# Key maximum taken pair by pair into a PSUM bank, with the engine orders rewritten

## Chip, cores and metric

The program runs on one core of one Trainium2 chip. The metric is the device time of one execution in microseconds (us). Three executions of the kernel before took 1970.22, 1972.08 and 1973.30 us; the median is 1972.08 us.

## What is computed

The reference is one gated cross-attention block and a small gated LoRA mixture behind it:

```
q = layernorm(x) @ wq          # x: 8 batches x 56 tokens x 512; 32 query heads of 128
k = ctx @ wk ; v = ctx @ wv    # ctx: 8 x 1500 x 512; 8 key heads, each shared by 4 query heads
q, k = rope(q), rope(k)
attn = softmax(q k^T / sqrt(128) + mask)      # over the 1500 keys
x = x + tanh(g0) * ((attn v) @ wo)
x = x + tanh(g1) * ffn(layernorm(x))          # 4 LoRA experts, top 2
```

Everything is float32. Large products are made of three fp32r matmuls (hi*hi, hi*lo, lo*hi), for which each operand is split into a high and a low part.

## The kernel before

Three stages follow one another: the query projection (up to about 120 us), the attention stage (to about 1835 us for its first 63 steps), and the output projection with the expert layer. The change is in the attention stage. It has 64 steps, one for each batch `b` (8) and key head `g` (8). In a step 1500 keys stand in 12 tiles of 125 keys on partitions, taken as 6 pairs, and the 4 heads x 56 queries are 224 columns.

The work of a step, by the names used in the order tables:

- `S0`..`S5` (TensorE, `scores`): the scores of one pair of tiles, 6 matmuls into one of two PSUM banks (`t_banks`). A bank is free again when VectorE has read it (semaphore `t_free`).
- `mask0`..`mask5` (VectorE, `add_mask`, L1059): adds the mask and stores the pair in `weights` (SBUF, 125 x 448).
- `max0`, `max1` (VectorE, L1068 and L1077): two row reductions over the stored pairs give `key_max` (125 x 224).
- `MT` (TensorE, L902) transposes `key_max` into `m_bank`; `rows` (VectorE, L1082) reduces it to one maximum for each query; `MB` (TensorE, L909) spreads that back over the key partitions into `m_bank`.
- `sub0`..`sub2` (VectorE, L1089) subtract it, `exp0`..`exp2` (ScalarE, L800) exponentiate, `add1`..`add5` and `total` (GpSimd, L718, L725) add the weights up.
- `PV0`..`PV5` (TensorE, L929) multiply the weights with `v`, `SUM` (L918) spreads the sums, `inv` and `norm` (VectorE, L1096, L1102) divide. A `z` in front of a word marks work of the step before: PV, SUM, inv and norm run one step late.
- `K00`..`K23` (TensorE, L840) project the next step's keys in 3 chunks of 4 parts; `swap` and `K` (ScalarE, L752, L757), `cos`, `sin`, `rot` (VectorE, L1000, L1005, L1014) and `klo` (GpSimd, L687) rotate and split them. `V00`..`V51` (TensorE, L857) project values for a pair of key heads, `V` on ScalarE (L774) stores them.
- `C0`..`C11` and `B0`, `B1` in the last step of a batch: the context and the mask of the next batch are transposed through the same two `t_banks` (L868, L877), with `C` on ScalarE (L761) and on VectorE (L1019) behind.

Nothing is scheduled at run time. Each engine executes a list written out in the tables `PE_STEP`, `ACT_STEP`, `DVE_STEP` and `POOL_STEP`, one entry for each kind of step. The kinds of a batch are zero, odd, even, odd, even, odd, pre, turn; in the last batch the last two are pre_last and last. An engine runs its list in order and waits at an instruction until its semaphores are reached, so whatever stands behind a waiting instruction waits too. A fill of a `t_banks` bank has to have the same place among the fills in the TensorE table and in the VectorE table.

Of the kernel before, what the change touches and what calls it, by code (L numbers as in the profile page):

```python
# [11 lines left out]
AX_X = mybir.AxisListType.X  # L12
# [4 lines left out]
HKV, REP, DH = 8, 4, 128  # L17
# [8 lines left out]
ST = 125  # L26
# [509 lines left out]
def attention_part(nc, ctx, query, shared, cT, ctx_in, mask, wo, q_dram, attn_dram):  # L536
# [50 lines left out]
    steps2 = HKV // 2  # L587
    ADDS = PT - 1
    GROUP = PT // GROUPS
    SHIFTED = PT - GROUP  # L590

    def c_stage_ready(eng, b, m):

# [930 lines left out]
```

## Time and profile before

| | |
|---|---|
| median of three runs | 1972.08 us |
| profiled execution, its own time | 1971.75 us |
| its span, first to last instruction | 1970.0 us |
| TensorE (PE) busy | 1910.2 us, 97% |
| VectorE (DVE) busy | 1530.4 us, 78% |
| ScalarE (ACT) busy | 781.0 us, 40% |
| GpSimd (POOL) busy | 747.5 us, 38% |
| granted TensorE clock, mean | 0.995 |

Matmuls overlap in the trace: one is shown for 0.27 us while the next starts 0.11 us after it. A busy share of 97% therefore does not say how many matmul slots were lost; the distance between the starts of neighbouring matmuls does. PEld is the loading of weights for the matmul behind it, and its waits are shown apart.

### The profile page before, as it was taken

What the parts mean: (1) busy time and instruction counts of PE and PEld (TensorE: products, weight loads), DVE (VectorE), ACT (ScalarE), POOL (GpSimd) and SP (SyncE); (2) the same over time, 40 slices, a digit from 0 to 9 for tenths busy, and PEclk for the clock granted to TensorE, in tenths of its full rate; (3) what the DMA queues carried; (4) which work ended last, traced back from release to release, by engine and by line L of the source; (5) the groups of instructions that cost most, each with busy time, mean ns of one, the idle gap of its engine ahead of it and who ended that gap; (6) DMA issues with size and microseconds to landing.
All of it is one profiled execution on the core that took longest, in us unless ns stands there. A gap on an engine that the chain in (4) does not pass through costs nothing. (4 is left out here: it accounts for less than half of the span.)

```text
span 1970.0 us, 32471 instructions
## 1 busy us (share of the span) xinstructions
PE 1910.2 (97%) x12452; PEld 1776.9 (90%) x12452; DVE 1530.4 (78%) x1822; ACT 781.0 (40%) x1242; POOL 747.5 (38%) x611
## 2 busy tenths in 40 slices
PE   7989999999999999999999999999999999999798
PEld 7879999999999998999899998999899999999786
DVE  6767788788787888778878788787887878778644
ACT  5643334433344334344343343334433334334422
POOL 5513334433343343443244432444234442344500
PEclk9999999999999999999999999999999999999998
DMA  6620001100010001000010001000010000100270
GB/s 223 246 93 22 23 11 34 41 26 10 21 38 30 17 8 41 31 26 10 24 36 31 16 8 41 31 26 10 24 42 25 16 13 21 48 10 8 85 227 19
DMA packets 54806, 84.31 MB, mean 43 GB/s; under 512 B 11684, under 2 KB 30244, under 8 KB 54664
## 3 DMA queue, kind: packets, MB, share of 16 engines
q1 hardware_dynamic: 53656, 75.92, 12.0%
q10 hardware_dynamic: 1008, 6.42, 0.8%
q8 instruction: 98, 1.61, 0.3%
q14 instruction: 44, 0.36, 0.1%
HBM read 66.62 MB, written 15.71 MB: 42 GB/s over the span
## 5 line engine op out<-in xcount | busy, mean ns | idle before, releaser
L687 POOL TENSOR_TENSOR k_lo<-k_work,k_hi 128x500 fp32r<-128x500 f32 x192 | 255.9, 1333 | 569.0 <-ACT k_hi L757 540.9
L752 ACT ACTIVATE k_work<-low_banks 64x500 f32<-64x500 f32 x384 | 223.7, 582 | 581.3 <-PE low_banks L840 575.9
L857 PE MATMUL low_banks<-wv_hi,cT_hi 128*125 128x256 f32 x1536 | 438.3, 285 | 0.0
L857 PE MATMUL low_banks<-wv_lo,cT_hi 128*125 128x256 f32 x1536 | 431.8, 281 | 0.0
L857 PE MATMUL low_banks<-wv_hi,cT_lo 128*125 128x256 f32 x1536 | 431.3, 281 | 0.0
L1059 DVE TENSOR_TENSOR weights<-t_banks,mask_keys 125x448 f32<-125x448 f32 x384 | 236.0, 622 | 162.6 <-PE t_banks L891 161.5
L929 PE MATMUL o_bank<-weights,v 125*128 125x224 f32 x1536 | 337.2, 353 | 0.0
L718 POOL TENSOR_TENSOR key_sum<-key_sum,weights 125x448 f32<-125x448 f32 x256 | 313.7, 1225 | 32.0 <-POOL key_sum L718 1.8
L840 PE MATMUL low_banks<-cT_hi,wk_hi 128*128 128x500 f32 x768 | 322.6, 420 | 0.0
L840 PE MATMUL low_banks<-cT_lo,wk_hi 128*128 128x500 f32 x768 | 298.3, 388 | 0.0
L840 PE MATMUL low_banks<-cT_hi,wk_lo 128*128 128x500 f32 x768 | 298.3, 388 | 0.0
L857 PEld LDWEIGHTS low_banks<-wv_hi,cT_lo 128*125 128x125 f32 x1536 | 285.4, 186 | 3.6
L857 PEld LDWEIGHTS low_banks<-wv_hi,cT_hi 128*125 128x125 f32 x1536 | 285.4, 186 | 3.4
L857 PEld LDWEIGHTS low_banks<-wv_lo,cT_hi 128*125 128x125 f32 x1536 | 285.3, 186 | 0.0
L929 PEld LDWEIGHTS o_bank<-weights,v 125*128 125x128 f32 x1536 | 273.5, 190 | 3.8
L718 POOL TENSOR_TENSOR key_sum<-weights 125x448 f32<-125x448 f32 x64 | 74.3, 1162 | 490.4 <-ACT weights L800 490.1
L891 PE MATMUL t_banks<-q_hi,k_hi 128*125 128x224 f32 x768 | 234.8, 306 | 3.1 <-DVE weights L1059 1.2
L1089 DVE TENSOR_TENSOR weights<-weights,m_bank 125x896 f32<-125x896 f32 x192 | 199.9, 1079 | 31.5 <-PE m_bank L909 31.5
L1068 DVE TENSOR_REDUCE weights<-weights 125x224 f32<-125x1792 f32 x64 | 214.5, 3352 | 1.7
L891 PE MATMUL t_banks<-q_lo,k_hi 128*125 128x224 f32 x768 | 209.1, 272 | 0.0
L891 PE MATMUL t_banks<-q_hi,k_lo 128*125 128x224 f32 x768 | 209.0, 272 | 0.0
L1005 DVE TENSOR_TENSOR k_work<-k_work,k_tables 128x500 f32<-128x500 f32 x192 | 165.0, 859 | 46.3 <-ACT k_work L752 46.3
(140 smaller groups left out, 3081.4 us busy)
## 6 DMA issues: line engine op xcount, KB each, us to landing
stage<-in_ctx_dram SPq DMA_DIRECT2D x72, 250.0 KB
attn_by_head<-o_sum SPq DMA_DIRECT2D x65, 112.0 KB, 1.7
wq_raw<-in_L_xattn_wq_dram SPq DMA_DIRECT2D x7, 1024.0 KB, 7.2
q_raw<-q_by_head SPq DMA_DIRECT2D x64, 112.0 KB, 2.0
head_rows<-in_ctx_dram SPq DMA_DIRECT2D x24, 250.0 KB
stage<-in_L_xattn_wo_dram SPq DMA_DIRECT2D x4, 1024.0 KB, 5.3
k_work<-in_L_xattn_wo_dram SPq DMA_DIRECT2D x4, 1024.0 KB, 5.5
q_by_head<-head_rows ACTq DMA_DIRECT2D x4, 896.0 KB, 6.1
```

The source lines that it names most:

```text
L687: nc.gpsimd.tensor_tensor(k[1][:, c * SC:(c + 1) * SC], k_rot[:, s], f32(k[0][:, c * SC:(c + 1) * SC]), ALU.subtract).then_inc(k_lo, 1)
L718: nc.gpsimd.tensor_tensor(key_sum[:, :, :], so_far, pair_weights(n, j), ALU.add).then_inc(p_added, 1)
L752: nc.scalar.activation(k_swap[lo * HALF:(lo + 1) * HALF, s], k_banks[(1 - lo) * HALF:(2 - lo) * HALF, s, 0:SC], ACT.Copy).then_inc(k_swapp ...
L840: mm = nc.tensor.matmul(k_banks[:, s, 0:SC], w[0][a][:, d, g * DH:(g + 1) * DH], cT[m][:, d, c * SC:(c + 1) * SC], start=(d == 0 and n == ...
L857: mm = nc.tensor.matmul(v_banks[0:ST, v_item(pair, m) % 2, t * PAIR:(t + 1) * PAIR], cT[a][:, d, tile * ST:(tile + 1) * ST], w[1][mv][:, d ...
L891: mm = nc.tensor.matmul(t_banks[0:ST, item % 2, t * GQ:(t + 1) * GQ], k[a][:, tile], q[m][:, :], start=(n == 0), stop=(n == len(PASSES) - 1))
L929: mm = nc.tensor.matmul(o_acc, v[n // 2 % 2][:, 2 * j + t, (n % 2) * DH:(n % 2 + 1) * DH], probs[:, t], start=(j == 0 and t == 0), stop=(j ...
L1005: nc.vector.tensor_tensor(k_swap[:, s], k_swap[:, s], tables[:, 1, c * SC:(c + 1) * SC], ALU.mult).then_inc(k_sined, 1)
L1059: nc.vector.tensor_tensor(pair_weights(n, j).rearrange(four, h=REP), t_banks[0:ST, item % 2, 0:2 * GQ].rearrange("p (t h s) -> p t h s", t ...
L1068: nc.vector.tensor_reduce(weights[:, NT, :], pair_weights(b * HKV + g, 0, SHIFTED).rearrange("p t q -> p q t"), AX_X, ALU.max).then_inc(ma ...
L1089: nc.vector.tensor_tensor(group, group, max_b[:, None, :].broadcast_to([ST, 2 * GROUP, GQ]), ALU.subtract).then_inc(p_shifted, 1)
```

## The change

Instead of two reductions over stored tiles, the running maximum is updated pair by pair. `max1` takes the elementwise maximum of pairs 0 and 1 and writes it (125 x 448) into `m_bank`; `max2` to `max4` take the maximum of `m_bank` and the next pair and write it back; `max5` writes into `key_max`, now two halves of 224 columns; `half` takes the maximum of these halves. `MT` reads the first half. `weights` loses its spare tile, in which the partial maximum stood. `MT` no longer waits for `p_shifted`; `max1` waits for it instead.

```diff
-    weights = sb("weights", [ST, 2 * NT + 1, GQ])
+    weights = sb("weights", [ST, 2 * NT, GQ])
-    key_max = sb("key_max", [ST, GQ])
+    key_max = sb("key_max", [ST, 2, GQ])
+    max_so_far = m_bank[0:ST, 0:2 * GQ].rearrange("p (t q) -> p t q", t=2)
...
-            nc.vector.tensor_reduce(weights[:, NT, :], pair_weights(b * HKV + g, 0, SHIFTED).rearrange("p t q -> p q t"),
-                                    AX_X, ALU.max).then_inc(max_begun, 1)
...
-            nc.vector.tensor_reduce(key_max[:, :], weights[:, first:first + 2 * GROUP + 1, :].rearrange("p t q -> p q t"),
-                                    AX_X, ALU.max).then_inc(max_ready, 1)
+        def max_part(b, g, j, last):
+            n = b * HKV + g
+
+            dve.wait_ge(t_free, t_item(b, g, "S", j, last) + (RING + 1))
+            if j == 1:
+                so_far = pair_weights(n, 0)
+                if n:
+
+                    dve.wait_ge(p_shifted, n * GROUPS)
+            else:
+                so_far = max_so_far
+                dve.wait_ge(max_steps, n * (PT - 1) + (j - 1))
+            out = key_max[:, :, :] if j == PT - 1 else max_so_far
+            nc.vector.tensor_tensor(out, so_far, pair_weights(n, j), ALU.max).then_inc(max_steps, 1)
+
+        def max_half(n):
+            dve.wait_ge(max_steps, (n + 1) * (PT - 1))
+            nc.vector.tensor_tensor(key_max[:, 0], key_max[:, 0], key_max[:, 1], ALU.max).then_inc(max_ready, 1)
```

All tables but `first` are rewritten (`last` on VectorE alone). Of TensorE's, the even and the turn step; of ScalarE's, pre_last, whose `K2` moves behind `V5` and `exp2`:

```diff
 PE_STEP
-    "even": ("zPV0 S0 S1 zPV1 S2 zPV2 S3 S4 zPV3 K00 zPV4 zPV5 S5 zSUM K01 K02 K03 MT K10 K11 K12 MB V30 K13 V31 "
-             "V40 K20 K21 K22 K23 V41 V50 V51"),
+    "even": ("S0 S1 zPV0 S2 S3 zPV1 S4 zPV2 zPV3 S5 K00 zPV4 K01 K02 K03 zPV5 MT K10 K11 K12 MB zSUM K13 K20 K21 "
+             "V30 V31 V40 V41 K22 K23 V50 V51"),
-    "turn": ("S0 S1 zPV0 S2 S3 zPV1 C0 S4 C1 zPV2 zPV3 S5 zPV4 C2 C3 zPV5 zSUM B0 B1 K00 C4 K01 K02 K03 MT C5 C6 "
+    "turn": ("S0 S1 zPV0 S2 S3 zPV1 C0 S4 zPV2 C1 S5 zPV3 zPV4 C2 C3 zPV5 zSUM MT B0 B1 K00 C4 K01 K02 K03 C5 V00 "
 ACT_STEP
-    "pre_last": "Q swap0 swap1 exp0 K0 exp1 exp2 V3 swap2 wo0 K1 V4 K2 V5 attn0",
+    "pre_last": "Q swap0 swap1 K0 V3 exp0 exp1 swap2 wo0 K1 V4 V5 exp2 K2 attn0",
```

VectorE's program in an even step (head 2 of the first batch), from the first mask to `rows`, before:

```order
L1059 TENSOR_TENSOR weights<-t_banks,mask_keys 125x448 [waits p_weighed,p_added,t_ready,t_free]
L1059 TENSOR_TENSOR weights<-t_banks,mask_keys 125x448 [waits t_ready] x3
L1068 TENSOR_REDUCE weights<-weights 125x224 [waits key_max_ready,t_free]
L1059 TENSOR_TENSOR weights<-t_banks,mask_keys 125x448 [waits t_ready] x2
L1077 TENSOR_REDUCE key_max<-weights 125x224 [waits max_begun,t_free]
L1082 TENSOR_REDUCE row_max<-m_bank 112x2 [waits max_turned]
```

and after, where L1057 is the mask, L1074 a maximum of a pair and L1078 the maximum of the halves:

```order
L1057 TENSOR_TENSOR weights<-t_banks,mask_keys 125x448 [waits p_weighed,p_added,t_ready,t_free]
L1057 TENSOR_TENSOR weights<-t_banks,mask_keys 125x448 [waits t_ready] x4
L1074 TENSOR_TENSOR m_bank<-weights 125x448 [waits p_shifted,t_free]
L1074 TENSOR_TENSOR m_bank<-m_bank,weights 125x448 [waits max_steps,t_free] x3
L1057 TENSOR_TENSOR weights<-t_banks,mask_keys 125x448 [waits t_ready]
L1074 TENSOR_TENSOR key_max<-m_bank,weights 125x448 [waits max_steps,t_free]
L1078 TENSOR_TENSOR key_max<-key_max 125x224 [waits max_steps]
L1082 TENSOR_REDUCE row_max<-m_bank 112x2 [waits max_turned]
```

Behind the last mask stood one reduction; now two shorter operations stand there, and four maxima stand between the fifth mask and the sixth.

VectorE's program in the turn step of the first batch, from the first mask to the mask copies, before (L1019 is the low part of a context tile):

```order
L1059 TENSOR_TENSOR weights<-t_banks,mask_keys 125x448 [waits p_weighed,p_added,t_ready,t_free]
L1059 TENSOR_TENSOR weights<-t_banks,mask_keys 125x448 [waits t_ready] x3
L1019 TENSOR_TENSOR cT_lo<-t_banks,cT_hi 128x4x125 [waits c_hi_ready]
L1059 TENSOR_TENSOR weights<-t_banks,mask_keys 125x448 [waits t_ready]
L1068 TENSOR_REDUCE weights<-weights 125x224 [waits key_max_ready,t_free]
L1019 TENSOR_TENSOR cT_lo<-t_banks,cT_hi 128x4x125 [waits c_hi_ready]
L1059 TENSOR_TENSOR weights<-t_banks,mask_keys 125x448 [waits t_ready]
L1019 TENSOR_TENSOR cT_lo<-t_banks,cT_hi 128x4x125 [waits c_hi_ready] x2
L1024 COPY mask_keys<-t_banks 125x336 [waits t_ready] x2
L1077 TENSOR_REDUCE key_max<-weights 125x224 [waits max_begun,t_free]
```

and after, its first twelve rows (L1017 is the low part of a context tile):

```order
L1057 TENSOR_TENSOR weights<-t_banks,mask_keys 125x448 [waits p_weighed,p_added,t_ready,t_free]
L1057 TENSOR_TENSOR weights<-t_banks,mask_keys 125x448 [waits t_ready]
L1074 TENSOR_TENSOR m_bank<-weights 125x448 [waits p_shifted,t_free]
L1057 TENSOR_TENSOR weights<-t_banks,mask_keys 125x448 [waits t_ready]
L1074 TENSOR_TENSOR m_bank<-m_bank,weights 125x448 [waits max_steps,t_free]
L1057 TENSOR_TENSOR weights<-t_banks,mask_keys 125x448 [waits t_ready]
L1074 TENSOR_TENSOR m_bank<-m_bank,weights 125x448 [waits max_steps,t_free]
L1017 TENSOR_TENSOR cT_lo<-t_banks,cT_hi 128x4x125 [waits c_hi_ready]
L1057 TENSOR_TENSOR weights<-t_banks,mask_keys 125x448 [waits t_ready]
L1074 TENSOR_TENSOR m_bank<-m_bank,weights 125x448 [waits max_steps,t_free]
L1017 TENSOR_TENSOR cT_lo<-t_banks,cT_hi 128x4x125 [waits c_hi_ready]
L1057 TENSOR_TENSOR weights<-t_banks,mask_keys 125x448 [waits t_ready]
```

The long reduction that stood between the fifth mask and the second context tile is gone, and two maxima now stand in front of the fourth mask, where none stood.

TensorE's program around `MT` in the same even step, before:

```order
L840 MATMUL low_banks<-cT_hi,wk_hi 128x500
L840 MATMUL low_banks<-cT_hi,wk_lo 128x500
L840 MATMUL low_banks<-cT_lo,wk_hi 128x500
L902 MATMUL m_bank<-ident,key_max 112x125 x2
L840 MATMUL low_banks<-cT_hi,wk_hi 128x500
```

and after (L841 is the key projection, L927 PV, L900 `MT`):

```order
L841 MATMUL low_banks<-cT_hi,wk_hi 128x500
L841 MATMUL low_banks<-cT_hi,wk_lo 128x500
L841 MATMUL low_banks<-cT_lo,wk_hi 128x500
L927 MATMUL o_bank<-weights,v 128x224 x2
L900 MATMUL m_bank<-ident,key_max 112x125 x2
L841 MATMUL low_banks<-cT_hi,wk_hi 128x500
```

`MT` now stands behind the last PV, and `SUM` has gone from in front of it to behind `MB`.

## Rows read from the trace of the kernel before

**Rows 1.** Windows, one whole batch: busy us and instructions of each engine

```profile
556.96:775.72 218.76, 215.67 (x1448) 201.97 (x1447) 177.10 (x207) 85.59 (x140) 84.49 (x73) 1.00 0.08 25
```

**Rows 2.** Waits of TensorE: us in total, times, longest

```profile
PEld m_bank L902 <- DVE key_max L1077: 18.1, 17, 1.2
...
PEld t_banks L868 <- DVE cT_lo L1019: 16.3, 21, 1.1
PEld t_banks L891 <- DVE weights L1059: 6.0, 17, 1.3
```

**Rows 3.** Timeline of PE, even step around MT: start, us, [idle before]

```profile
620.04 0.39 PE L840 MATMUL low_banks<-cT_hi,wk_lo 128*128 128x500 f32 x1
620.27 0.39 PE L840 MATMUL low_banks<-cT_lo,wk_hi 128*128 128x500 f32 x1
621.29 0.43 PE L902 MATMUL m_bank<-ident,key_max 125*112 125x125 f32 x2 [0.62 <-DVE key_max L1077]
```

**Rows 4.** Timeline of PE, odd step, from S1 to S2

```profile
637.72 0.27 PE L891 MATMUL t_banks<-q_lo,k_hi 128*125 128x224 f32 x1
638.09 0.37 PE L891 MATMUL t_banks<-q_hi,k_hi 128*125 128x224 f32 x1
```

**Rows 5.** Timeline of PE, turn step, from PV1 to C2

```profile
525.83 0.93 PE L929 MATMUL o_bank<-weights,v 125*128 125x224 f32 x4
526.60 0.59 PE L868 MATMUL t_banks<-ident,stage 125*128 125x125 f32 x4
...
527.46 0.27 PE L891 MATMUL t_banks<-q_hi,k_lo 128*125 128x224 f32 x1
527.57 0.27 PE L891 MATMUL t_banks<-q_lo,k_hi 128*125 128x224 f32 x1
528.59 0.65 PE L868 MATMUL t_banks<-ident,stage 125*128 125x125 f32 x4 [0.75 <-DVE cT_lo L1019]
...
532.93 1.18 PE L868 MATMUL t_banks<-ident,stage 125*128 125x125 f32 x8 [0.76 <-DVE cT_lo L1019]
```

**Rows 6.** Groups of VectorE by form: busy us, mean ns, idle before

```profile
L1059 DVE TENSOR_TENSOR weights<-t_banks,mask_keys 125x448 f32<-125x448 f32 x384 | 236.0, 622 | 162.6 <-PE t_banks L891 161.5
L1068 DVE TENSOR_REDUCE weights<-weights 125x224 f32<-125x1792 f32 x64 | 214.5, 3352 | 1.7
L1077 DVE TENSOR_REDUCE key_max<-weights 125x224 f32<-125x1120 f32 x64 | 137.5, 2149 | 1.1
L1029 DVE TENSOR_TENSOR q_lo<-q_raw,q_hi 128x224 fp32r<-128x224 f32 x64 | 44.4, 693 | 8.9 <-ACT q_hi L767 8.9
L1102 DVE TENSOR_TENSOR o_sum<-o_bank,inv_b 128x224 f32<-128x224 f32 x64 | 24.6, 385 | 1.1
L514 DVE TENSOR_TENSOR q_banks<-q_banks,q_cos_t 128x448 f32<-128x448 f32 x32 | 19.9, 623 | 0.0
```

**Rows 7.** Timeline of DVE and POOL, one even step: the same operation twice

```profile
625.61 0.67 DVE L1005 TENSOR_TENSOR k_work<-k_work,k_tables 128x500 f32<-128x500 f32 x1
...
629.70 1.66 DVE L1005 TENSOR_TENSOR k_work<-k_work,k_tables 128x500 f32<-128x500 f32 x1
...
629.67 2.70 POOL L718 TENSOR_TENSOR key_sum<-key_sum,weights 125x448 f32<-125x448 f32 x2
```

**Rows 8.** Timeline of PE and DVE, start of a zero step

```profile
556.96 0.26 PE L891 MATMUL t_banks<-q_hi,k_hi 128*125 128x224 f32 x1
...
557.86 0.62 DVE L1059 TENSOR_TENSOR weights<-t_banks,mask_keys 125x448 f32<-125x448 f32 x1 [0.28 <-PE t_banks L891]
```

**Rows 9.** Timelines around the last step: ACT, POOL, PE

```profile
1836.37 0.61 ACT L757 ACTIVATE k_hi<-k_work 128x500 fp32r<-128x500 f32 x1
...
1836.07 2.48 POOL L687 TENSOR_TENSOR k_lo<-k_work,k_hi 128x500 fp32r<-128x500 f32 x2 [4.13 <-ACT k_hi L757]
...
1852.47 0.71 PE L1182 MATMUL low_banks<-cT_hi,wk_hi 128*128 128x448 f32 x1 [7.97 <-POOL cT_lo L699]
```

**Rows 10.** Groups of ScalarE by form

```profile
L800 ACT ACTIVATE weights<-weights 125x896 f32<-125x896 f32 x192 | 179.9, 949 | 36.3 <-DVE weights L1089 33.9
```

More of the change, by code:

```diff
@@ L90 @@
 DVE_STEP = {
[13 rows of a table removed]
[13 rows of a table added]
+             "inv norm"),
     "first": "C2 C3 C4 C5 C6 C7 cos0 C8 sin0 C9 rot0 C10 C11 cos1 sin1 rot1 Q B0 B1 cos2 sin2 rot2",
@@ L576, in attention_part @@
     t_ready, t_hi, t_free = sem("t_ready"), sem("c_hi_ready"), sem("t_free")
-    max_begun, max_ready, max_turned, rows_ready, max_spread = (
-        sem(n) for n in ("max_begun", "key_max_ready", "max_turned", "row_max_ready", "max_spread"))
+    max_steps, max_ready, max_turned, rows_ready, max_spread = (
+        sem(n) for n in ("max_steps", "key_max_ready", "max_turned", "row_max_ready", "max_spread"))
     p_shifted, p_exp, p_added, p_weighed = (
@@ L589, in attention_part @@
     GROUP = PT // GROUPS
-    SHIFTED = PT - GROUP
     def c_stage_ready(eng, b, m):
@@ L601, in pair_weights @@
     def pair_weights(n, j, count=1):
-        first = 2 * j if n % 2 == 0 else NT + 1 + 2 * ((j + PT - SHIFTED) % PT)
+        first = (n % 2) * NT + 2 * j
         return weights[:, first:first + 2 * count, :]
@@ L897, in turn_max @@
             pe.wait_ge(max_ready, n + 1)
-            if n:
-                pe.wait_ge(p_shifted, n * GROUPS)
             for h in range(HALVES):
-                mm = nc.tensor.transpose(m_bank[0:ROWS, h * ST:(h + 1) * ST], key_max[:, h * ROWS:(h + 1) * ROWS], ident[0:ST, 0:ST])
+                mm = nc.tensor.transpose(m_bank[0:ROWS, h * ST:(h + 1) * ST], key_max[:, 0, h * ROWS:(h + 1) * ROWS], ident[0:ST, 0:ST])
             mm.then_inc(max_turned, 1)
@@ L1061, in add_mask @@
                                     mask_keys[:, j, :, None, :].broadcast_to([ST, 2, REP, SQ]), ALU.add).then_inc(t_free, 1)
-        def max_begin(b, g, last):
-            dve.wait_ge(t_free, t_item(b, g, "S", SHIFTED - 1, last) + (RING + 1))
-            if b * HKV + g:
-                dve.wait_ge(max_ready, b * HKV + g)
-            nc.vector.tensor_reduce(weights[:, NT, :], pair_weights(b * HKV + g, 0, SHIFTED).rearrange("p t q -> p q t"),
-                                    AX_X, ALU.max).then_inc(max_begun, 1)
-        def max_end(b, g, last):
-            n = b * HKV + g
-            dve.wait_ge(t_free, t_item(b, g, "S", PT - 1, last) + (RING + 1))
-            dve.wait_ge(max_begun, n + 1)
-            first = 2 * SHIFTED if n % 2 == 0 else NT
-            nc.vector.tensor_reduce(key_max[:, :], weights[:, first:first + 2 * GROUP + 1, :].rearrange("p t q -> p q t"),
-                                    AX_X, ALU.max).then_inc(max_ready, 1)
+        def max_part(b, g, j, last):
+            n = b * HKV + g
+            dve.wait_ge(t_free, t_item(b, g, "S", j, last) + (RING + 1))
[11 more added lines that the diff above has]
+            nc.vector.tensor_tensor(key_max[:, 0], key_max[:, 0], key_max[:, 1], ALU.max).then_inc(max_ready, 1)
         def max_rows(n):
@@ L1113, in step @@
                 if what == "max":
-                    (max_end if j else max_begin)(b, g, last)
+                    max_part(b, g, j, last)
+                if what == "half":
+                    max_half(n)
                 if what == "rows":
```

56 rows, old and new, of tables (ACT_STEP, DVE_STEP, PE_STEP, POOL_STEP) are left out of this document.

## Prediction, written before the changed kernel was run

> **What bounds the kernel now.** I looked at the busy shares first: TensorE 97%, VectorE 78%, the others at or under 40%. The windows of one batch [rows 1] then say where a gain can lie: of 218.76 us TensorE is shown busy for 215.67, while VectorE works for 177.10. So taking work off VectorE is worth nothing in itself. The change can only give back slots in which TensorE waits for VectorE. The waits list of TensorE names them [rows 2]: `MT` for `key_max`, 17 times; the context transposes for the low parts, 21 times; the scores for a bank that a mask still reads, 17 times, one of them 1.3 us in the first step.
>
> What a wait costs is read from starts, since matmuls overlap. In the even step the key projections start 0.23 us apart, then `MT` starts 1.02 us after the last one [rows 3]: 0.79 us lost, though the page prints 0.62. There are 16 such, two in each batch, in the even steps alone. In the odd step S2 starts 0.37 us after the last matmul of S1, where 0.11 is the usual distance [rows 4, 5]: 0.26 us lost, and I found this 14 times. In the turn step C1 starts 1.02 us after a score instead of 0.11 [rows 5], 0.91 lost, and C2 waits as long by its printed idle time (0.76 beside 0.75). Seven turn steps with two such make 12.7 us; the other waits for low parts in [rows 2] are short, and I allow 0.5 us in each turn step for them.
>
> TensorE's losses to VectorE in the attention stage are then 16 x 0.79 = 12.6, 14 x 0.26 = 3.6, 7 x (1.82 + 0.5) = 16.2, one `MT` wait of the first step, of about 1.1 by the mean in [rows 2] (18.1 / 17), and 1.3 in front of a score in the first step: 34.8 us. That is the most that the change can win there.
>
> **The new operations.** Both reductions go: 3352 + 2149 = 5501 ns in each step [rows 6]. Five maxima of 448 columns and one of 224 come. `max2` to `max4` read one operand from PSUM and one from SBUF and write PSUM. L514 is the same form and size: 623 ns; the mask, PSUM and SBUF into SBUF, takes 622. I take 0.62 for these three and for `max5`. `max1` reads two operands from SBUF. L1005 has that form with 500 columns: 0.67 us when GpSimd is idle, 1.66 while GpSimd adds [rows 7]. Scaled to 448 columns that is 0.60 to 1.49; I take 0.8, since `max1` overlaps with a GpSimd operation only in some kinds of step. `half` lies between 385 (L1102, one operand from PSUM) and 693 ns (L1029, two from SBUF, the mean with and without GpSimd); I take 0.5. The sum is 4 x 0.62 + 0.8 + 0.5 = 3.8 us against 5.5, so VectorE has 1.7 us less to do in a step; behind the last mask it is 0.62 + 0.5 = 1.1 us instead of 2.15.
>
> The rows show 1792 columns reduced in 3352 ns, 1.9 ns for each, and 448 columns multiplied in 623 ns, 1.4 for each, its fixed part included [rows 6]. The Trainium skill speaks against this change in "VectorE: DVE Perf Modes", section "Rules for kernel authors": minimise the count of operations. Two become six here; with the fixed part of about 151 cycles at 0.96 GHz that the same page measured for an fp32 tensor_tensor (section on the TRN2 errata), four more would be an estimate of 0.6 us more in a step, where the rows give 1.7 less. The page's figure lies inside each duration already, so the sum goes by the rows.
>
> **Even step.** I walk the new order with durations from rows: S 0.65 us (6 x 0.11), a PV pair 0.77 (525.83 to 526.60 [rows 5]), a K part of three matmuls 0.68, a context tile 0.43. A mask starts 0.90 us after its S starts [rows 8], so 0.25 after S ends. S0 at 0; S5 ends at 7.0; K00, PV4, K01 to K03 and PV5 follow, and `MT` comes up at 11.2. On VectorE the fifth mask ends at 5.7, `max1` to `max4` at 8.4, the sixth mask at 9.0, `max5` at 9.6, `half` at 10.1. `MT` finds `key_max` ready with 1.1 us to spare: 12.6 us gained. With `max1` at its upper end 0.4 are left, and still no wait.
>
> **Odd, zero and pre steps.** In the odd step K00 stands between PV0 and S2, so S2 is no longer behind a mask that just ends: 3.6 us gained. `half` ends at 11.5 and `MT` comes at 12.5. In the zero step it is 12.9 against 14.3, in the pre step 12.3 against 14.3. The tightest new place that I find is `MB` in the zero step: `rows` now stands behind `sin0` and `zinv` and ends at about 15.7, with `MB` at 15.9. I count these at nothing; a cover of 0.2 us that fails would cost some tenths eight times, at most 3 us.
>
> **Turn step.** Here two maxima stand ahead of the fourth mask. S4 needs the bank that this mask reads and comes up at 4.56; the mask ends at 4.8 with `max1` at its low end, at 5.4 with the high end: 0.3 to 0.9 us of new wait. C1 now has a PV pair more in front of it, and comes at 6.3, where C0's low part ends at 6.1 to 6.7: nothing or a little. S5 waits some 0.1, B1 some 0.1. The three-microsecond reduction that held back C1's low part is gone, so C2 and C3 do not wait. I take 0.8 us where 2.32 were, between 0.5 and 1.2. That gives 7 x 1.5 = 10.6 us (8 to 13).
>
> **First and last step.** The `MT` wait of the first step goes, 1.1 us; the 1.3 in front of S2 there stay, since the rotation of the first keys holds VectorE. In pre_last, ScalarE's `K2` [rows 9] now stands behind `V5` and `exp2` (0.95 us [rows 10]), some 1.4 us later. GpSimd did its low part right after the one before it, in 2.48 us for both; it now ends about 1.2 us later, and all that GpSimd does after it too: adds, total, and the low parts for the output projection, for which TensorE waits 7.97 us [rows 9]. This is on the path that sets the end: 1.2 us lost.
>
> **Sum.** 12.6 + 3.6 + 10.6 + 1.1 - 1.2 = 26.7 us. The profiled execution took 1971.75 us, 1.75 more than its span and 0.33 less than the median of the runs, so the two bases agree. 1971.75 - 26.7 = 1945.0 us.
>
> **Rivals.** (1) The maxima take more than their rows say, or stall one another. Each reads from PSUM what the one before wrote, in two steps of the chain with nothing between them, and no row shows such a chain. If one costs x more, `half` is 5x later. The slack is 1.1 us in 16 even steps, 1.0 in 24 odd, 1.4 in 8 zero steps, and in 7 turn steps all of 5x is added to the 0.8 that are left. The gain is eaten when 55 x 5x - 17.6 - 24 - 11.2 = 26.7, that is 5x = 1.45 and a maximum of 0.91 us. At 1.1 us (5x = 2.4) it is 55 x 2.4 - 52.8 = 79 us against 26.7: about 2024 us, slower. L514 in its own place, at 623 ns with PSUM read and written, speaks against it. (2) The turn step keeps its waits: with GpSimd busy each time, `max1` at 1.49 and each later SBUF read slow, S4, C1, S5 and B1 wait 2.3 together. Then 10.6 is gone: 1955.5 us. For it: the low part of the last key chunk runs on GpSimd early in that step. Against it: four operations would all have to be hit. (3) New waits in many steps pay back the gain. Exponentials now stand behind key copies on ScalarE, and key low parts ahead of the adds on GpSimd; 0.4 us in each of 64 steps would give 26 us: 1971, no change. By my walk the tightest are S4 in the turn step, which needs the last key chunk and has 0.8 us of slack, and S2 in the zero step, with 0.8 too; two kinds of step of seven, so 0.4 in every one is unlikely. (4) More is won than I count: no wait is left in the turn step, and the walk of the last step is too dark. 34.8 us less 1.3: 1938.
>
> **How the numbers follow.** Forecast 64%, rival 4 12%, rival 2 12%, rival 3 5%, rival 1 7%. The forecast's own range is 1938 to 1952, from the ends of the turn step, `MB` in the zero step and 0 to 2.5 us in the last. With rival 2 and most of rival 4 in, and half of the way to rival 3, the range is 1934 to 1958. A change of 0.2% (4 us) is about what a measurement of this kernel can tell. Faster by more than that: the forecast, rivals 2 and 4 and a little of the rest, 0.89. Within: 0.04. Slower: 0.07.
>
> **What would show it.** The waits list after should have no `MT` row for `key_max`, or a few tenths; an even step should be 0.8 us shorter from its first score to the next step's; the turn step should show one wait in front of S4 for the fourth mask and none of 0.75 in front of a context tile. VectorE should be busy some 105 us less. The maxima should be rows of about 620 ns, `max1` longer and mixed. TensorE's wait for the low parts ahead of the output projection should be about 9 us. I am wrong if the maxima stand at 0.9 or more, if `MT` still waits, or if a score waits for a low part of the keys.

## The result, and the profile after

The changed kernel took 1938.6 us (median of 4 runs, 1935.6 to 1939.3) against 1972.6 us before (1970.2 to 1973.3): 34.0 us less, ratio 0.983 with an interval of 0.981 to 0.984. The forecast was 1945.0 us in a range of 1934 to 1958. The profiled execution took 1939.1 us with a span of 1937.4, against 1971.75 and 1970.0, so the two profiles that are compared below are 32.6 us apart. The prediction had 26.7 for that.

The page's first part, busy us and share of the span:

```profile
PE 1899.7 (98%) x12452; PEld 1777.8 (92%) x12452; DVE 1386.1 (72%) x2078; ACT 774.2 (40%) x1242; POOL 749.9 (39%) x611
```

VectorE issues 256 instructions more (six for two in 64 steps) and yet works 144.3 us less than the 1530.4 of before. The windows of one whole batch, with the columns of [rows 1]:

```profile
547.19:761.45 214.26, 214.20 (x1449) 202.08 (x1447) 159.24 (x239) 84.72 (x140) 85.02 (x72) 1.00 0.08 26
```

TensorE has the same work in 4.50 us less, and there is no idle time left that the windows show. The waits of TensorE (total, times, longest), first its weight loads, then its matmuls, answer to [rows 2]:

```profile
PEld t_banks L892 <- DVE weights L1057: 4.0, 9, 1.3
PEld t_banks L869 <- DVE cT_lo L1017: 2.5, 3, 1.2
```

```profile
PE low_banks L1184 <- POOL cT_lo L700: 9.0, 1, 9.0
PE t_banks L892 <- DVE weights L1057: 1.2, 1, 1.2
```

The 18.1 us for `key_max` are gone. These lists are of the whole run, while [rows 2] counts the attention stage alone (over the whole run the kernel before has 19.0 us in 25 waits for the low parts and 6.6 in 18 for a mask). In the stage nothing is left of the 16.3 us for the low parts: the 2.5 stand ahead of it. Of the 6.0 us for a mask 3.4 are left there, in 8 waits. An even step around `MT`, on PE, is the counterpart of [rows 3]: `MT` starts 0.56 us after the start of three PV matmuls (three of 0.19), with no idle time in brackets.

```profile
609.22 0.73 PE L927 MATMUL o_bank<-weights,v 125*128 125x224 f32 x3
609.78 0.38 PE L900 MATMUL m_bank<-ident,key_max 125*112 125x125 f32 x2
609.92 0.47 PE L841 MATMUL low_banks<-cT_hi,wk_hi 128*128 128x500 f32 x1
```

The groups of VectorE by form (busy us, mean ns | idle before), beside those of [rows 6] and the operation of [rows 7]:

```profile
L1057 DVE TENSOR_TENSOR weights<-t_banks,mask_keys 125x448 f32<-125x448 f32 x384 | 237.5, 624 | 230.0 <-PE t_banks L892 183.3 <-POOL key_sum L719 44.5
...
L1003 DVE TENSOR_TENSOR k_work<-k_work,k_tables 128x500 f32<-128x500 f32 x192 | 135.6, 706 | 72.4 <-ACT k_work L753 72.4
...
L1074 DVE TENSOR_TENSOR m_bank<-m_bank,weights 125x448 f32<-125x448 f32 x192 | 121.2, 631 | 14.6 <-DVE m_bank L1074 0.9
...
L1074 DVE TENSOR_TENSOR m_bank<-weights 125x448 f32<-125x448 f32 x64 | 55.6, 869 | 1.1
L1074 DVE TENSOR_TENSOR key_max<-m_bank,weights 125x448 f32<-125x448 f32 x64 | 39.9, 624 | 4.2
L1027 DVE TENSOR_TENSOR q_lo<-q_raw,q_hi 128x224 fp32r<-128x224 f32 x64 | 33.2, 519 | 0.0
...
L1078 DVE TENSOR_TENSOR key_max<-key_max 125x224 f32<-125x224 f32 x64 | 25.1, 392 | 2.2
```

The four maxima that read the bank of the turns take 631 and 624 ns, `max1` 869, `half` 392: 3.78 us in a step, where 3.8 were forecast.

The turn step, first on PE and then on DVE (compare [rows 5]):

```profile
517.67 0.93 PE L927 MATMUL o_bank<-weights,v 125*128 125x224 f32 x4
518.44 0.59 PE L869 MATMUL t_banks<-ident,stage 125*128 125x125 f32 x4
519.09 0.37 PE L892 MATMUL t_banks<-q_hi,k_hi 128*125 128x224 f32 x1
...
519.84 0.93 PE L927 MATMUL o_bank<-weights,v 125*128 125x224 f32 x4
520.60 0.59 PE L869 MATMUL t_banks<-ident,stage 125*128 125x125 f32 x4
...
521.71 1.68 PE L927 MATMUL o_bank<-weights,v 125*128 125x224 f32 x8
523.23 1.02 PE L869 MATMUL t_banks<-ident,stage 125*128 125x125 f32 x8
```

```profile
516.46 0.63 DVE L1074 TENSOR_TENSOR m_bank<-weights 125x448 f32<-125x448 f32 x1
...
518.42 0.61 DVE L1057 TENSOR_TENSOR weights<-t_banks,mask_keys 125x448 f32<-125x448 f32 x1
519.07 0.63 DVE L1074 TENSOR_TENSOR m_bank<-m_bank,weights 125x448 f32<-125x448 f32 x1
519.69 0.68 DVE L1017 TENSOR_TENSOR cT_lo<-t_banks,cT_hi 128x500 fp32r<-128x500 f32 x1
```

C1 starts 0.76 us after the PV pair ahead of it, and C2 1.52 after two pairs: neither waits, where each lost 0.9 before. The fourth mask ends at 519.03, and S4 starts at 519.09, 0.65 after C0 starts, where the score behind the next tile, C1, starts after 0.36: this 0.3 is the one wait that the prediction expected there.

**Where the 32.6 us come from.** I took the distance of each TensorE start from the one before in the attention stage, less the usual distance of its kind. What is over is lost. The stage, from its first score to the first score of the last step, took 1713.2 us and takes 1678.3.

| lost by TensorE, us | before | after |
|---|---|---|
| `MT` in 16 even steps | 13.4 | 0 |
| S2 in 15 odd steps | 4.1 | 0 |
| 7 turn steps | 18.5 | 3.0 |
| first step | 2.7 | 1.4 |
| sum | 38.7 | 4.4 |

That is 34.3 us of the 34.9; the other 0.6 are in small gaps. From the first score of the last step to the end it took 135.0 us and now takes 137.5: 2.5 are given back. The start, up to the first score, is 0.2 shorter. The two outer parts are not as firm as the stage. In the profiles of the experiments below a step of one kind and one order repeats to some hundredths of a microsecond in nearly every case. But the start, which no experiment touches, took 120.7 to 124.2 us, and the part behind the first score of the last step took 135.3 (turn_masks_first) to 137.6 (turn_old) in kernels that have the last step of the changed one. The rest of the text takes these lines apart.

### The profile page after: what moved, and what is told of

It reads as the page before. It is cut to its first block and busy times, and to the rows that moved or that the text cites. A ratio compares the mean times of both kernels' runs of the same rounds, so it can differ in the third digit from the quotient of the medians.

```text
span 1937.4 us, 32856 instructions
## 1 busy us (share of the span) xinstructions
PE 1899.7 (98%) x12452; PEld 1777.8 (92%) x12452; DVE 1386.1 (72%) x2078; ACT 774.2 (40%) x1242; POOL 749.9 (39%) x611
## 5 line engine op out<-in xcount | busy, mean ns | idle before, releaser
L1057 DVE TENSOR_TENSOR weights<-t_banks,mask_keys 125x448 f32<-125x448 f32 x384 | 237.5, 624 | 230.0 <-PE t_banks L892 183.3
L927 PE MATMUL o_bank<-weights,v 125*128 125x224 f32 x1536 | 344.0, 353 | 0.0
L841 PE MATMUL low_banks<-cT_hi,wk_hi 128*128 128x500 f32 x768 | 322.0, 419 | 0.0
L719 POOL TENSOR_TENSOR key_sum<-key_sum,weights 125x448 f32<-125x448 f32 x256 | 298.3, 1165 | 31.4 <-POOL key_sum L719 0.4
L841 PE MATMUL low_banks<-cT_hi,wk_lo 128*128 128x500 f32 x768 | 298.9, 389 | 0.0
L841 PE MATMUL low_banks<-cT_lo,wk_hi 128*128 128x500 f32 x768 | 298.4, 389 | 0.0
L927 PEld LDWEIGHTS o_bank<-weights,v 125*128 125x128 f32 x1536 | 270.9, 190 | 4.5
L775 ACT ACTIVATE v<-low_banks 125x512 f32<-125x512 f32 x192 | 111.9, 588 | 223.3 <-PE low_banks L858 222.7
L801 ACT ACTIVATE weights<-weights 125x896 f32<-125x896 f32 x192 | 175.2, 941 | 32.0 <-DVE weights L1089 31.5
L1003 DVE TENSOR_TENSOR k_work<-k_work,k_tables 128x500 f32<-128x500 f32 x192 | 135.6, 706 | 72.4 <-ACT k_work L753 72.4
```

The source lines that it names most:

```text
L719: nc.gpsimd.tensor_tensor(key_sum[:, :, :], so_far, pair_weights(n, j), ALU.add).then_inc(p_added, 1)
L775: nc.scalar.activation(v[pair % 2][:, 2 * m:2 * m + 2, :], v_banks[0:ST, v_item(pair, m) % 2, :].rearrange("p (t n) -> p t n", t=2), ACT.C ...
L801: nc.scalar.activation(group, group, ACT.Exp).then_inc(p_exp, 1)
L841: mm = nc.tensor.matmul(k_banks[:, s, 0:SC], w[0][a][:, d, g * DH:(g + 1) * DH], cT[m][:, d, c * SC:(c + 1) * SC], start=(d == 0 and n == ...
L927: mm = nc.tensor.matmul(o_acc, v[n // 2 % 2][:, 2 * j + t, (n % 2) * DH:(n % 2 + 1) * DH], probs[:, t], start=(j == 0 and t == 0), stop=(j ...
L1003: nc.vector.tensor_tensor(k_swap[:, s], k_swap[:, s], tables[:, 1, c * SC:(c + 1) * SC], ALU.mult).then_inc(k_sined, 1)
```

## Experiments

Each ran beside the kernel before on one chip, in 3 rounds, or 5 where this is said. The experiments were spread over three chips, on which the kernel before took 1971.6, 1971.7 and 1972.0 us (medians), so times of different experiments can be compared.

**The operations without the orders.** PE, ACT and POOL keep the orders of before; in each DVE row `max0` becomes `max1 max2 max3` and `max1` becomes `max4 max5 half`, with the new code of the operations.

```
-    "even": ("mask0 mask1 mask2 mask3 max0 mask4 mask5 max1 rows sub0 cos0 ...
+    "even": ("mask0 mask1 mask2 mask3 max1 max2 max3 mask4 mask5 max4 max5 half rows sub0 cos0 ...
```

> The new maxima in the old orders: max0 is replaced by max1 max2 max3 in its place, max1 by max4 max5 half, and TensorE, ScalarE and GpSimd keep the tables of before. Theory A (the shorter chain behind the last mask does most of it): in the even step key_max is ready at about the time when MT comes up, so 12.6 us there and 1.1 in the first step go, and C2 in the turn step no longer waits (7 x 0.9 = 6.5); S2 in the odd step and C1 in the turn step keep their waits. 1972.6 - 20 = 1952.5 us, 1949 to 1956. Theory B (the orders do it): less than 8 us go, 1965 or more.

1953.1 us, ratio 0.991 (0.989 to 0.992): 18.5 us less than before, as expected. Weight loads of TensorE, by their waits over the whole run (before: 19.0, 18.1 and 6.6 us):

```profile
PEld t_banks L868 <- DVE cT_lo L1016: 10.8, 17, 1.2
PEld m_bank L899 <- DVE key_max L1077: 6.6, 16, 0.4
PEld t_banks L891 <- DVE weights L1056: 6.6, 18, 1.3
```

The 16 waits of `MT` are shorter but still there (0.15 us of lost start each), and so are S2's in the odd steps and more than half of the turn step's loss: it takes 33.3 us, where it took 34.5 before and takes 32.3 in the changed kernel (from its first matmul to that of the next step). The operations alone bring half of the gain.

**The orders without the operations.** The new tables, with the two old reductions: the first in the place of `max4`, the second in that of `half`.

```
-    "even": ("mask0 mask1 mask2 mask3 mask4 max1 max2 max3 max4 mask5 max5 half rows cos0 ...
+    "even": "mask0 mask1 mask2 mask3 mask4 max0 mask5 max1 rows cos0 ...
```

> The new orders with the two old reductions: max0 stands where max4 stood, max1 where half stood. Theory A: the orders are fitted to the short chain and lose by themselves. By the walk max1 ends 1.5 us behind MT in 24 odd steps, 0.7 in 16 even, 1.8 in 8 zero and 2 in 8 pre steps, and the turn step waits about 3: 36 + 11 + 14 + 16 + 21 = 98 us of waits in place of the 35 of before, so about 2035 us, 2010 to 2050. Theory B (the orders carry the gain): under 1960 us.

2039.0 us, ratio 1.034 (1.032 to 1.036): slower than before by 67 us, as theory A had it.

```profile
PEld m_bank L896 <- DVE key_max L1071: 86.9, 63, 2.9
```

`MT` waits in 63 of 64 steps. The new orders put it early, and this only pays if the maximum is early too. The gain is thus not a sum of two gains: one half alone gives 18.5, the other alone loses 67, both together win 34.

**The running maximum in SBUF.** Maxima 1 to 4 write `key_max` instead of the bank.

```
-    max_so_far = m_bank[0:ST, 0:2 * GQ].rearrange("p (t q) -> p t q", t=2)
+    max_so_far = key_max[:, :, :]
```

> The changed kernel, with the running maximum kept in key_max (SBUF) instead of the PSUM bank, so that all five maxima read two SBUF operands. Theory A (the bank is not what matters, the slack of 1.0 to 1.4 us in each step covers the contention with GpSimd): within 5 us of 1938.6. Theory B (the bank matters, since an operation with two SBUF operands takes 1.49 us beside GpSimd): two or three maxima in a step take 0.9 us longer, past the slack by 0.8 us in 64 steps: about 1985 us.

1949.2 us, ratio 0.988 (0.986 to 0.990): 10.6 us more than the changed kernel, between the two expectations, so that neither holds. The group on VectorE, and the wait that appears:

```profile
L1074 DVE TENSOR_TENSOR key_max<-key_max,weights 125x448 f32<-125x448 f32 x256 | 208.7, 815 | 18.8 <-DVE key_max L1074 0.9
```

```profile
PEld m_bank L900 <- DVE key_max L1078: 8.0, 24, 0.3
```

815 ns instead of 629 is 0.74 us more in a step on VectorE. The trace shows where they come from: 152 of the 256 maxima ran while GpSimd was idle and took 624 ns in the mean, the 104 that overlapped with a GpSimd operation took 1095. GpSimd's last addition (L726) takes 925 instead of 760 ns. Three places pay for it: each of the 24 odd steps waits at `MT` (0.2 us, 5.0 in all), each of the 7 turn steps is 0.57 us longer (4.0 in all, most of it at S4 and S5), and the last step loses 1.0. That `m_bank` is PSUM is worth about a third of the gain.

**How much slack is there.** The maximum with pair 4 is taken three times more (which changes no value), 1.95 us more in a step.

```
+            if j == PT - 2:
+                for again in range(3):
+                    dve.wait_ge(max_steps, n * STEPS_OF_MAX + (j + again))
+                    nc.vector.tensor_tensor(out, max_so_far, pair_weights(n, j), ALU.max).then_inc(max_steps, 1)
```

> The changed kernel, with the maximum of pair 4 taken three times more in each step (same form, same result): 1.9 us more on VectorE ahead of key_max. Theory A (slack of 1.0 us in 24 odd steps, 1.1 in 16 even, 1.4 in 8 zero, 2.0 in 8 pre, none to speak of in 7 turn steps, and nothing else is late): 21 + 13 + 4 + 0 + 13 = 51 us, 1989 us, 1975 to 2000. Theory B (VectorE at 72% has room, nothing is lost): 1939. Theory C (VectorE's work counts in full): 64 x 1.9 = 120, 2059 us.

2005.3 us, ratio 1.017 (1.015 to 1.018), that is 66.7 us more than the changed kernel: the wait returns, and is dearer than the 51 us of theory A, whose range ended at 2000.

```profile
PEld m_bank L901 <- DVE key_max L1083: 60.5, 56, 1.9
...
PEld m_bank L908 <- DVE row_max L1087: 6.8, 7, 1.0
```

By starts an odd step is 1.2 us longer, an even one 1.0 (1.3 in two of 16), a zero step 1.6 (half of it at `MT`, half at `MB`), a pre step 0.2, a turn step 1.2, in front of C2. So the slack is 1.95 less these: 0.75, 0.95, 0.35, 1.75 and 0.75. (The expectation of the next run quotes the values of odd and even steps the wrong way round; its sum does not use them.) The walk of the prediction gave 1.0, 1.1, 1.4 at `MT` in the zero step with `MB` tight at 0.2, and 2.0. It was good to 0.25 us except in the zero step, where the tight place that it named decides. For the turn step it gave no slack to what is added behind S4, and there are 0.75. Against theory A the odd steps cost 28 us instead of 21, the zero steps 13 instead of 4, and the turn steps 8 instead of 13.

**One repetition**, 0.65 us more in a step, 5 rounds (same edit with `range(1)`).

> The changed kernel, with the maximum of pair 4 taken once more in each step, 0.65 us. From max_again_3 (1.95 us more cost 1.0 in an odd, 1.2 in an even, 1.6 in a zero, 0.2 in a pre, 1.2 in a turn step) the slack is 0.95, 0.75, 0.35, 1.75 and 0.75 us. Theory A (below the slack nothing is lost): 0.3 us in the zero steps alone, 8 x 0.3 = 2.4, 1941 us, 1938.6 to 1942. Theory B (cost is in proportion, 66.7 / 3): 1961 us.

1940.3 us, ratio 0.984 (0.983 to 0.986), as expected; it lies 1.7 us above the changed kernel. Only the zero step is longer, 25.65 instead of 25.38 us (0.57 us more in the very first one):

```profile
PEld m_bank L908 <- DVE row_max L1087: 2.8, 7, 0.4
```

37 us more work on VectorE (busy 1423.5 us, against 1386.1) thus cost some 2 us: as long as it stays within the slack it is hidden.

**The old operations, `MT` later.** The kernel before, with one row of PE changed: K10 and K11 stand ahead of `MT`, and K13 ahead of V30.

```
-    "even": ... zSUM K01 K02 K03 MT K10 K11 K12 MB V30 K13 V31
+    "even": ... zSUM K01 K02 K03 K10 K11 MT K12 K13 MB V30 V31
```

> The kernel before with one edit of TensorE's order: in the even steps MT stands behind K10 and K11, two key parts of 0.68 us later, and MB behind K13. Operations and all other orders are those of before. Theory A (the 16 waits of MT need no new operation, only other work in front of them): 12.6 us go, 1959.5 us, 1957 to 1963. Theory B (what MT waits for comes back behind it, since MB, the shifts and the exponentials move back with it): 1966 us or more.

1954.2 us, ratio 0.991 (0.989 to 0.992): 17.5 us less than before, where 12.6 were expected.

```profile
PEld m_bank L902 <- DVE key_max L1077: 1.2, 1, 1.2
PEld t_banks L891 <- DVE weights L1059: 2.2, 3, 1.3
```

One wait for `key_max` is left, that of the first step. But the waits for a bank fell as well, from 18 to 3 over the whole run: the 15 of S2 in the odd steps are gone, 4.1 us. They were the end of the step before. VectorE's masks stand behind the rotation of the last key chunk (L1014), here in the odd step of [rows 4], whose first score starts at 635.76, before:

```profile
636.83 0.68 DVE L1014 TENSOR_TENSOR k_work<-low_banks,k_work 128x500 f32<-128x500 f32 x1
637.42 1.23 DVE L1059 TENSOR_TENSOR weights<-t_banks,mask_keys 125x448 f32<-125x448 f32 x2
```

and in old_mt_later, where it starts at 632.81:

```profile
632.55 0.68 DVE L1014 TENSOR_TENSOR k_work<-low_banks,k_work 128x500 f32<-128x500 f32 x1
633.72 0.62 DVE L1059 TENSOR_TENSOR weights<-t_banks,mask_keys 125x448 f32<-125x448 f32 x1 [0.48 <-PE t_banks L891]
```

The first mask starts 1.66 us after the first score before, held by the rotation, and 0.91 here. Which of the moved parts made the rotation early was not tested apart. The turn step's waits (18.8 us of weight loads for `cT_lo`, 19.0 before) stay. So one edit on PE recovers as much as the new operations do.

**Both.** The operations of `ops_only` and this PE row.

> ops_only with the one edit of TensorE's even step as in old_mt_later. Theory A (the new maxima and the later MT mend the same 16 waits, and only what ops_only had left goes): 2.4 us behind MT and 3.9 in front of S2 of the odd steps, 1953.1 - 6.3 = 1946.8 us. Theory B (the two gains of 18.5 and 17.5 us add up): 1935.6 us.

1943.5 us, ratio 0.986 (0.985 to 0.988). The two gains do not add up (18.5 + 17.5 would be 36, measured 28.5), since both remove the same `MT` waits. The time lies between the two theories, 3.3 us under A: the stage is 8.0 us shorter than in ops_only, where A had 6.3. What is left are the turn steps, at 33.3 us each as in ops_only, and the first step:

```profile
PEld t_banks L868 <- DVE cT_lo L1016: 10.8, 17, 1.2
...
PEld t_banks L891 <- DVE weights L1056: 2.2, 3, 1.3
```

**The turn step of before in the changed kernel.** All four turn rows as before, with the DVE row of `ops_only`.

```
-    "turn": ("S0 S1 zPV0 S2 S3 zPV1 C0 S4 zPV2 C1 S5 zPV3 zPV4 C2 C3 ...
+    "turn": ("S0 S1 zPV0 S2 S3 zPV1 C0 S4 C1 zPV2 zPV3 S5 zPV4 C2 C3 ...
```

> The changed kernel, with the turn step's rows of before in all four tables (max1 max2 max3 in the place of max0, max4 max5 half in that of max1); all other steps are the changed ones. In ops_only such a turn step lost 1.6 us to low parts and banks, in the changed kernel 0.4. Theory A (the turn step's new order is a term of its own, larger than the prediction had it): 7 x 1.15 = 8 us more than 1938.6, 1946.7, 1945 to 1949. Theory B (the maxima alone mended the turn step): within 3 us of 1938.6.

1946.9 us, ratio 0.987 (0.986 to 0.989): 8.3 us more than the changed kernel, as expected, all of it in the turn steps (34.1 instead of 32.9 us each, from first score to first score).

```profile
PEld t_banks L869 <- DVE cT_lo L1017: 11.6, 17, 1.2
```

C1 waits 0.91 us in each again, although VectorE has the short operations. That wait comes from the place of C1 so close behind C0, whose high part ScalarE and whose low part VectorE must make first, and not from the reduction: it goes when a PV pair stands between S4 and C1. The C2 wait fell from 0.93 to 0.19: that one was the reduction.

**Masks ahead of maxima in the turn step**, 5 rounds. It tests whether the 0.30 us left in front of S4 can be had.

```
-    "turn": ("mask0 mask1 max1 mask2 max2 mask3 max3 C0 mask4 max4 C1 ...
+    "turn": ("mask0 mask1 max1 mask2 mask3 max2 C0 mask4 max3 max4 C1 ...
```

> The changed kernel, with max2 moved behind mask3 and max3 behind mask4 in VectorE's turn step. Theory A (S4 no longer waits 0.30 us for mask3, but C1's and S5's banks depend on C0's low part and the mask behind it, which are bound by ScalarE and do not move): the wait moves from S4 to C1 or S5 and nothing is gained, within 1 us of 1938.6. Theory B (the wait in front of S4 is simply lost time): 7 x 0.3 = 2.1 us less, 1936.5.

1938.4 us, ratio 0.983 (0.982 to 0.985): no change. S4 waits no more. C1 waits in its place (it starts 0.92 us after the PV pair instead of 0.76), and S5 by another 0.12 us:

```profile
519.33 0.93 PE L927 MATMUL o_bank<-weights,v 125*128 125x224 f32 x4
520.25 0.65 PE L869 MATMUL t_banks<-ident,stage 125*128 125x125 f32 x4
```

The turn step stays at 32.9 us: the wait moved.

**The last step: `K2` where it was**, 5 rounds.

```
-    "pre_last": "Q swap0 swap1 K0 V3 exp0 exp1 swap2 wo0 K1 V4 V5 exp2 K2 attn0",
+    "pre_last": "Q swap0 swap1 K0 V3 exp0 exp1 swap2 wo0 K1 V4 K2 V5 exp2 attn0",
```

> The changed kernel, with K2 back in front of V5 and exp2 in ScalarE's pre_last. Theory A (K2's place costs what GpSimd is late by in the last step, 1.1 to 1.3 us, and the longer idle time of TensorE costs up to 1 us more at the lower clock behind it): 1936.3 to 1937.5 us. Theory B (the last step is bound by something else): 1938.6.

1937.5 us, ratio 0.983 (0.981 to 0.984), 1.1 us under the changed kernel. The direction is the expected one, but a difference of 1.1 is not clear of the runs' scatter. The profile shows GpSimd's part of it: TensorE's wait for the low parts is shorter, and the output projection starts 18.00 us after the first score of the last step instead of 18.74.

```profile
PE low_banks L1184 <- POOL cT_lo L700: 8.5, 1, 8.5
```

**And VectorE makes the attention's low parts** of the first output projection block in place of GpSimd, 5 rounds.

```
-    "last": "attn0 attn1 attn2 attn3 add1 add2 add3 add4 add5 total",       (POOL)
+    "last": "add1 add2 add3 add4 add5 total",
...
+    "last": ("... max5 half zinv znorm A0 rows sub0 sub1 sub2 O1 inv norm"),  (DVE)
...
+                if what == "A":
+                    attn_low(nc, dve, nc.vector, shared, j, 0)
```

> k2_early, and in the last step the low part of the first head group's attention output is made by VectorE in one operation behind norm, instead of by GpSimd in four of 1.1 us behind its work on wo. VectorE is idle there for 12 us. Theory A (the output projection starts as soon as both low parts are there): TensorE's wait of 9.0 us shrinks to 3.5 to 4.5, 4 to 6 us less and up to 2 more if the clock stays at its upper level: 1930 to 1933.5 us. Theory B (the loads of the following head groups are what is late, so the end does not move): 1936 or more.

1935.7 us, ratio 0.981 (0.980 to 0.983): the lowest median of all, 2.9 under the changed kernel, but not the 1930 to 1933.5 expected. Its runs (1934.3 to 1936.6) overlap with those of the changed kernel (1935.6 to 1939.3). The wait and the operation that it ends on, GpSimd's low parts of the output weights:

```profile
PE low_banks L1186 <- POOL wk_lo L696: 5.8, 1, 5.8
```

```profile
1809.29 6.86 POOL L696 TENSOR_TENSOR wk_lo<-stage,wk_hi 128x512 fp32r<-128x512 f32 x4
```

In k2_early these four operations took 5.08 us. Here VectorE subtracts beside them (L1169, 2.41 us from 1812.61), and they take 6.86: the wait could only fall to 5.8. The output projection starts 2.7 us earlier in the step than in k2_early. But in this profile TensorE stayed at its lower clock for 5.5 us of work instead of 3.4, and from there to the end it took 118.6 us instead of 116.0, so that the two profiles are only 0.7 us apart (1934.9 and 1935.6).

## Why the prediction was right, point by point

**The sum.** Both the direction and the mechanism held, and the number fell into the range. But every term of the gain was set too low: 26.7 us were forecast for what is 32.6 between the two profiles. By terms: `MT` 12.6 against 13.4, S2 3.6 against 4.1, the turn steps 10.6 against 15.5, the first step 1.1 against 1.3, nothing against 0.6 in small gaps and 0.2 at the start, and at the end a loss of 1.2 against 2.5.

**The bound.** That VectorE's share is worth nothing in itself holds: max_again_1 gives it back 37 us and loses about 2. That the gain is in lost starts of TensorE holds too. They were counted at 34.8 us, "the most that the change can win there", and are 38.7 for the same four places; the stage alone became 34.9 shorter, so this was no bound.

**`MT` in the even steps, 12.6 us.** The table has 13.4. It is gone, but the runs show that the new operations were not needed for it: old_mt_later removes all 16 waits with the old reductions. The prediction put all of it on the change as a whole and is not wrong, but the change holds two remedies for one wait. Its sign, an even step 0.8 us shorter, holds from first matmul to first matmul. From first score to first score, as the prediction worded it, the step is only 0.2 to 0.3 us shorter, because `zPV0` (0.6 us) now stands behind the first score and not ahead of it.

**S2 in the odd steps, 3.6 us.** 4.1 measured, in 15 steps: the prediction found 14 and missed the one in the first batch. The cause that it gave, K00 between PV0 and S2, was not needed. In the changed kernel the first mask of an odd step ends 1.53 us after the first score starts, where it ended after 2.27 before; S2 starts at 2.74, and by the durations would come up at about 1.9 without K00. Here too two remedies are in one change, and old_mt_later shows that the earlier rotation alone does it.

**The operations.** `max2` to `max5` 0.62 forecast, 0.63 measured; `max1` 0.8 against 0.87; `half` 0.5 against 0.39. The maxima do not stall one another: repeated in max_again_3, 192 more such operations have a mean of 632 ns. Rival 1, the slower one, falls with this. Its arithmetic of slack gives 55 x 1.95 - 52.8 = 54 us for max_again_3, and 66.7 were measured: the zero and odd steps have less slack than assumed, and the turn step has some.

**VectorE busy 105 us less** was the one sign that failed: it is 144.3 us less (1530.4 to 1386.1). The operations answer for 110 of these (352.0 to 241.8). Two operations with both operands in SBUF that nothing was done to more than fill the rest: `sin` (L1005, now L1003) from 165.0 to 135.6, and `q_lo` (L1029, now L1027) from 44.4 to 33.2, together 40.6 us; others, the masks among them, took a little more. This is the work of the orders: in ops_only, with the old ones, the two stay at 164.7 and 44.4, and in orders_only, with the old reductions, they are 134.2 and 33.2. The traces show why. Before, 111 of the 192 `sin` overlapped with a GpSimd operation and took 996 ns in the mean, the other 81 took 672; after, 47 overlap. It moved no end, as VectorE is not the bound.

**The turn step is the mis-sized term**: 7 x 1.5 = 10.6 us forecast, 15.5 measured, and with it 4.9 of the 5.9 us by which the sum is off. It failed on both sides. What was lost before is 18.5 / 7 = 2.64 us for each, not 2.32: the short waits for low parts, allowed 0.5, are 0.8 (0.29 in front of C after `MB`, 0.27 within C, 0.24 within B). What is left is 0.43, not 0.8, of it 0.30 before S4 and 0.13 in B. The walk had S4 waiting 0.3 to 0.9 as `max1` takes its low or high end; it took 0.63, the low end. GpSimd was busy beside it, as rival 2 supposed, but there GpSimd paid:

```profile
516.52 1.69 POOL L688 TENSOR_TENSOR k_lo<-k_work,k_hi 128x500 fp32r<-128x500 f32 x1 [1.24 <-ACT k_hi L758]
```

The same operation takes 1.24 elsewhere (two in 2.48 [rows 9]). Rival 2 fell for that reason, and because the later maxima, with one operand in the bank, took 0.63 beside GpSimd's additions too. Who pays for such a meeting is taken up in the last section.

**First step.** 1.1 forecast, 1.3 measured; the 1.3 us before S2 stay, as said (1.2 in the waits).

**Last step, -1.2 us.** The profiles have 2.5, in two parts. The first matmul of the output projection starts 18.74 us after the first score of the last step, where it started after 17.48: 1.26 us, which is the forecast term. The wait for the low parts in front of it grew from 7.97 to 9.0 us, as the prediction said. `K2`'s place makes 0.7 of the 1.26 (k2_early starts it after 18.00). The rest comes with the operations and the other orders; ops_only, with the orders of before, starts it after 17.79.

The other 1.2 us lie behind that start, and 0.8 of them in a stretch at TensorE's lower clock level. In both kernels it ran on at that level (0.50 granted, 1.2 GHz) after the idle stretch, but for 4.2 us of work before and 6.1 now (PE busy in the first columns, clock as the first of the last three), first before, then after:

```profile
1852.47:1856.67 4.20, 4.20 (x11) 3.77 (x12) 0.00 (x0) 0.00 (x0) 0.00 (x0) 0.50 0.66 226
```

```profile
1818.30:1824.69 6.39, 6.08 (x17) 5.38 (x18) 0.42 (x1) 0.00 (x0) 0.06 (x1) 0.51 0.72 275
```

At the full level such a matmul takes 0.20 us, so 11 of them lose 2.0 and 17 lose 2.7: about 0.7 us more. This part cannot be laid to the change. turn_masks_first has the last step of the changed kernel and the same wait ahead of the projection (8.98 us), and there the low level ended after 3.0 us of work:

```profile
1818.45:1821.48 3.03, 3.03 (x8) 2.73 (x9) 0.00 (x0) 0.00 (x0) 0.00 (x0) 0.50 0.61 168
```

From the start of the projection to the end it took 116.6 us, against 118.8 in the changed kernel; behind the shorter wait of 8.0 to 8.3 us it took 117.0 (ops_only), 117.6 (before) and 118.7 (old_mt_later). So the term was sized right, and the other 1.2 us are within what profiles of one order differ by.

**Rival 4**, more won than counted, gave 1938 and comes nearest as a number: 1938.6. Half of it is true, more or less: the turn step keeps 0.43 us of waits and not none, but lost more before than was counted. Its other half, that the last step costs nothing, is not. That its number is the nearest is partly luck. Rival 3 has no trace: no score waits for a low part of the keys, and a zero, odd, even and pre step each come out the same to 0.02 us in every batch, the very first step apart.

**A version beyond the change.** `K2` early and the attention's low parts on VectorE has the lowest median, 1935.7, though its lead over k2_early and the changed kernel is not clear of the scatter. What TensorE still waits for there is GpSimd's low part of the output weights; to make that earlier was not tried.

## What to carry to other kernels

Measure waits of a pipelined engine by the distance of its starts, list them by place, and ask of each which of two remedies it needs: shorter work on the engine that is late, or later work on the one that waits. Here either one alone gave 18 us, both gave 28, and a fitted order kept its gain only as long as the operations that it was fitted to were there (67 us lost without them). A walk through the new order with durations from rows was good to some 0.25 us at `MT` in four kinds of step, and the place it called tight was the first to break. And compare two profiles stage by stage with a third of the same order: here a stage repeated to a tenth of a microsecond, while the part behind it differed by 2 us between kernels that are alike in it.

## What the runs showed of the hardware beyond that

Six VectorE operations were cheaper than two. A maximum over 448 columns with the running value read from and written to PSUM takes 631 ns, also when several stand one behind another (632 for the repeated ones). The same with everything in SBUF takes 815 in the mean: 624 when GpSimd is idle and 1095 when it is not. The Trainium skill, in "VectorE: DVE Perf Modes", section "Rules for kernel authors", asks for few operations where they are chained, and in the same table to restructure a `tensor_reduce` on a hot path; here the second advice decides, since the long reduction took 1.9 ns for each column that it took in (3352 / 1792) and a pair maximum takes 1.4 for each that it adds (631 / 448).

When VectorE and GpSimd meet on SBUF, the one that began later pays. In [rows 7] GpSimd's addition began at 629.67 and L1005 at 629.70, and it took 1.66 us instead of 0.67. In the turn step `max1` began at 516.46 and GpSimd's low part at 516.52: `max1` kept its 0.63, and the low part took 1.69 instead of 1.24. I counted it for the VectorE operations with both operands in SBUF that overlapped with just one GpSimd operation, in the profiles of before, after, max_in_sbuf and orders_only. In 151 cases VectorE had begun first: it took at most 0.01 us more than alone, and GpSimd's operation 0.32 us more in the mean. In 88 GpSimd had begun first: VectorE took 0.44 us more in the mean, and GpSimd's operation at most 0.02 more. Operations with one operand in PSUM do not pay at all: after, 454 masks and maxima of 448 columns overlapped with GpSimd and none took over 0.633 us. So the bank keeps the running maximum out of these meetings. In the last experiment GpSimd's four operations went from 5.08 to 6.86.
